# Local attention of a sandwich block on Trainium2: values projected with Wv times Wo, q and k for 256 tokens at a time, norms of four blocks at once

## The reference

```python
x  = hidden_states
gates = sigmoid(x @ Wg + bg);  gates /= gates.sum(-1) + 1e-6
win = xw[:, widx]                         # windows of 64 tokens, one every 32
q, k, v = win @ Wq + bq, win @ Wk + bk, win @ Wv + bv
win_ctx = softmax(q k^T / 4) @ v          # reshaped to rows, first L rows kept
combined = concat(comp_out * g0, sel_out * g1, win_out * g2)
out = norm(0.5 * (combined @ Wo + bo) + 0.5 * x)
```

## Time and profile before

| | |
|---|---|
| median of 3 runs | 1918.43 us (1913.34 to 1921.14) |
| profiled execution | 1920.51 us, span 1918.7 us |
| busy PE, DVE, ACT, POOL | 1676.2, 1261.9, 926.7, 908.5 us |
| TensorE's mean granted clock | 0.941 of full |
| HBM | 18 GB/s over the span |

### The profile page before, as it was taken

How to read it: one execution, slowest core, us unless ns; L and a number is a source line. 1 busy time by engine, 2 the same in 40 slices (tenths; PEclk the granted TensorE clock), 3 DMA queues, 4 the chain that set the end, 5 groups by cost and what they waited for, 6 DMA issues and landing times.

```text
span 1918.7 us, 37804 instructions
## 1 busy us (share of the span) xinstructions
PE 1676.2 (87%) x10522; PEld 1285.8 (67%) x10522; DVE 1261.9 (66%) x3658; ACT 926.7 (48%) x2530; POOL 908.5 (47%) x1070
## 2 busy tenths in 40 slices
PE   3778677999289999999969999399999999789997
PEld 1222366887168787787757778277787877678876
DVE  3666342766478778787645555388788887656765
ACT  1110112554268778788821222178778787711211
POOL 4100031666465555555435554465555555346665
PEclk8788787999699999999989999699999999989999
DMA  4100001021300000000010000200000000001011
GB/s 120 61 1 0 1 0 46 31 68 66 90 3 6 5 4 5 5 4 5 6 60 11 9 8 11 63 4 6 5 4 5 5 4 5 8 23 44 22 43 44
DMA packets 53430, 43.79 MB, mean 23 GB/s; under 512 B 9580, under 2 KB 51840, under 8 KB 53376
## 3 DMA queue, kind: packets, MB, share of 16 engines
q1 hardware_dynamic: 53376, 43.15, 7.2%
HBM read 26.37 MB, written 8.39 MB: 18 GB/s over the span
## 4 chain that ended last, share of the span: by engine, by line
PE 73%; DVE 6%; SPq 6%; DMA 5%; POOL 4%; issue 3%; ACT 2%; POOLq 1%; DVEq 0%; ACTq 0%; PEldq 0%; PEld 0%
PE bank L1446 7%; PE bank L1532 7%; PE bank L1500 6%; PE bank L1459 5%; PE bank L1374 5%; PE bank L1593 5%; PE bank L1594 5%; PE bank L1595 5%; PE bank L1376 5%; PE bank L1375 5%; SPq L465 4%; PE bank L1398 3%; PE bank L1214 3%; DMA x_in<-in_L_attn_hidden_states 2%; POOL h_lo L743 2%
## 5 line engine op out<-in xcount | busy, mean ns | idle before, releaser
L686 POOL TENSOR_TENSOR rnorm<-sumsq,neg_half 128x8 f32<-128x8 f32 x128 | 210.9, 1648 | 139.8 <-DVE sumsq L1941 139.8
L1008 ACT ACTIVATE prob<-prob,neg_max 128x256 f32<-128x256 f32 x512 | 260.9, 516 | 2.3 <-DVE neg_max L2022 2.2
L1127 ACT ACTIVATE gelu_sb<-bank,b_sb 114x512 f32<-114x512 f32 x96 | 66.2, 689 | 350.8 <-PE bank L1595 350.8
L700 POOL TENSOR_TENSOR qk_cos<-qk_cos,qk_sin 128x512 f32<-128x512 f32 x128 | 163.5, 1278 | 125.3 <-DVE qk_cos L1904 122.9
L784 POOL TENSOR_TENSOR act_lo<-act_full,act_hi 114x512 fp32r<-114x512 f32 x96 | 127.0, 1323 | 177.8 <-PE bank L1610 102.5
L1374 PE MATMUL bank<-wqkv_hi,hT_hi 128*128 128x512 f32 x384 | 177.6, 462 | 3.7 <-DVE hT_lo L1890 1.9
L1593 PE MATMUL bank<-h_hi,w_hi 128*114 128x512 f32 (+1 forms) x384 | 156.5, 407 | 20.9 <-POOL h_lo L743 11.0
L1376 PE MATMUL bank<-wqkv_hi,hT_lo 128*128 128x512 f32 x384 | 154.4, 402 | 0.0
L1375 PE MATMUL bank<-wqkv_lo,hT_hi 128*128 128x512 f32 x384 | 154.0, 401 | 0.0
L1594 PE MATMUL bank<-h_hi,w_lo 128*114 128x512 f32 (+1 forms) x384 | 153.5, 400 | 0.0
L2191 DVE SCALAR_TENSOR_TENSOR act_full<-bank,b_sb,gelu_sb 114x512 f32<-114x512 f32 x96 | 71.0, 739 | 125.4 <-PE bank L1595 125.4
(11 more groups left out here) (225 smaller groups left out, 4224.7 us busy)
## 6 DMA issues: line engine op xcount, KB each, us to landing
x_in<-in_L_attn_hidden_states SPq DMA_DIRECT2D x16, 512.0 KB, 3.4
x_scratch<-x_in SPq DMA_DIRECT2D x8, 512.0 KB, 4.2
f_x<-x_scratch SPq DMA_DIRECT2D x8, 512.0 KB, 4.1
out<-f_y SPq DMA_DIRECT2D x8, 512.0 KB, 3.0
hs_attn<-x_sb SPq DMA_DIRECT2D x16, 254.0 KB
hs_ffn<-x_sb SPq DMA_DIRECT2D x64, 63.5 KB
raw<-in_L_ffn_wqkv SPq DMA_DIRECT2D x2, 1536.0 KB, 6.7
raw<-in_L_ffn_w SPq DMA_DIRECT2D x2, 1364.0 KB
```

Of the source, the lines that this page charges most:

```text
L686: pool.tensor_tensor(rnorm[:, part * HEADS:(part + 1) * HEADS], sumsq[:, which * HEADS:(which + 1) * HEADS], neg_half[:, 0:HEADS], ALU.pow ...
L1008: act.activation(prob[:, h], prob[:, h], ACT.Exp, bias=neg_max[:, h:h + 1], scale=-1.0, accum_out=psums[:, h:h + 1]).then_inc(exped, 1)
```

## The change

1. Before phase 2, `W' = Wv Wo3` (`wp_sb`) and `b' = bv Wo3` (`bp_bc`) are computed once: Wv is turned by PE, copied by ACT, multiplied, and copied. PE waits for it before it goes on. `bv` is loaded once more, as a column.
2. In phase 3 the values are `x W'`, straight from `xnT`, so the product with Wo and its copy fall away, and so does the copy of x. p stays unweighed; gate over row sum multiplies the result when it is added (`win_add_up`).
3. q and k are made in units of 288 tokens (four blocks and 32 more), one unit of q or k and one half of its channels per step.
4. Most buffers are doubled. The loops are written out: 32 + 16 steps, each engine with its own list.
5. Norms: POOL makes the scales for four blocks at once (128x4), and also a shift, minus mean times scale. ACT applies both norms as scale and bias. The sum with x0 is one POOL operation of 128x1024 per group. DVE keeps the moments.
6. SP has three buffers for x0. It stores group g as soon as its sum is made, then shifts group g - 2, then loads x0 of group g + 1.
7. For the first layer the sine table goes into rows of `hs_ffn` instead of `pT`.

```diff
+            sp.dma_start(bv_col[:], col(bv)).then_inc(w_loaded, 16)
...
-            sp.dma_start(x_in[:, 0], group_of(x0_b, 0)).then_inc(x0_loaded, 16)
-            sp.wait_ge(x0_loaded, 16)
-            sp.dma_start(x_in[:, 1], group_of(x0_b, 1)).then_inc(x0_loaded, 16)
-            def move_group(g, i):
+            for g in range(3):
+                sp.dma_start(x0_in[:, g], group_of(x0_b, g)).then_inc(x0_loaded[g], 16)
+            def store_x1(g):
+                sp.wait_ge(x1_made, g + 1)
+                sp.dma_start(group_of(x1_dram, g), x0_in[:, g % 3]).then_inc(x1_stored[g % 3], 16)
+            def move_group(g):
                 sp.wait_ge(x_made, (g + 1) * GB)
-                sp.dma_start(hs_attn[1:P, bass.ds(g * GB + g // GPB, GB), :],
-                             x_sb[0:P - 1, bass.ds(g * GB, GB), P:D]).then_inc(hs_moved, 16)
-                sp.dma_start(hs_attn[0:1, bass.ds(g * GB + g // GPB + 1, GB), :],
-                             x_sb[P - 1:P, bass.ds(g * GB, GB), P:D]).then_inc(hs_moved, 16)
-                sp.dma_start(group_of(x1_dram, g), x_in[:, i]).then_inc(x1_stored, 16)
-            with sp.Fori(0, NG // 2 - 1) as u:
-                for i in range(2):
-                    g = u * 2 + i
-                    move_group(g, i)
-                    sp.wait_ge(x1_stored, 16 * (g + 1))
-                    sp.wait_ge(x0_loaded, 16 * (g + 2))
-                    sp.dma_start(x_in[:, i], group_of(x0_b, g + 2)).then_inc(x0_loaded, 16)
-            move_group(NG - 2, 0)
-            sp.wait_ge(x1_stored, 16 * (NG - 1))
-            move_group(NG - 1, 1)
-            sp.wait_ge(x1_stored, 16 * NG)
+                at = g * GB + g // GPB
+                sp.dma_start(hs_attn[1:P, at:at + GB, :], x_sb[0:P - 1, g * GB:(g + 1) * GB, P:D]).then_inc(hs_moved, 16)
+                sp.dma_start(hs_attn[0:1, at + 1:at + 1 + GB, :], x_sb[P - 1:P, g * GB:(g + 1) * GB, P:D]).then_inc(hs_moved, 16)
+            for g in range(NG + 2):
+                if g < NG:
+                    store_x1(g)
+                if g >= 2:
+                    move_group(g - 2)
+                    if g + 1 < NG:
+                        sp.wait_ge(x1_stored[(g - 2) % 3], 16 * ((g - 2) // 3 + 1))
+                        sp.dma_start(x0_in[:, (g + 1) % 3], group_of(x0_b, g + 1)).then_inc(x0_loaded[(g + 1) % 3], 16)
+            for i in range(3):
+                sp.wait_ge(x1_stored[i], 16 * len(range(i, NG, 3)))
...
-            def x1_norm_root(b):
-                inverse_root(f_mv1[:, 1:2], f_r[:], 1e-5, x1_aggr, b + 1, x1_step, b + 1, x1_root, 1)
-            double_norm_scale(0)
-            double_norm_scale(1)
-            with pool.Fori(0, NB - 2) as b:
-                x1_norm_root(b)
-                double_norm_scale(b + 2)
...
+            def sum_scales(g):
+                i = g % 2
+                pool.wait_ge(m_aggr, GB * (g + 1))
+                if g >= 2:
+                    pool.wait_ge(m_norm, GB * (g - 1))
+                var = m_mv[:, i, :, 1]
+                pool.tensor_scalar(m_t[:, 0], var, 0.25, 1e-6, ALU.mult, ALU.add).then_inc(m_step, 1)
+                pool.tensor_scalar(m_t[:, 1], var, 0.25, None, ALU.mult).then_inc(m_step, 1)
+                pool.wait_ge(m_step, 9 * g + 2)
+                pool.tensor_tensor(m_t[:, 0], m_t[:, 0], neg_half[:, 0:GB], ALU.pow).then_inc(m_step, 1)
...
+            def make_x1(g):
+                pool.wait_ge(m_norm, GB * (g + 1))
+                pool.wait_ge(x0_loaded[g % 3], 16 * (g // 3 + 1))
+                pool.tensor_tensor(x0_in[:, g % 3], x0_in[:, g % 3], xs_st[:], ALU.add).then_inc(x1_made, 1)
+            def x1_scales(g):
+                i = g % 2
+                pool.wait_ge(x1_aggr, GB * (g + 1))
+                if g >= 2:
+                    pool.wait_ge(x_made, GB * (g - 1))
+                pool.tensor_scalar(f_r[:, i], f_mv1[:, i, :, 1], 1e-5, None, ALU.add).then_inc(x1_step, 1)
+                pool.wait_ge(x1_step, 3 * g + 1)
+                pool.tensor_tensor(f_r[:, i], f_r[:, i], neg_half[:, 0:GB], ALU.pow).then_inc(x1_step, 1)
+                pool.wait_ge(x1_step, 3 * g + 2)
+                pool.tensor_tensor(f_shift[:, i], f_mv1[:, i, :, 0], f_r[:, i], ALU.mult).then_inc(x1_step, 1)
+                pool.wait_ge(x1_step, 3 * g + 3)
+                pool.tensor_scalar(f_shift[:, i], f_shift[:, i], -1.0, None, ALU.mult).then_inc(x1_root, 1)
+            for n in range(NB + 16):
+                g, r = divmod(n, GB)
+                if r == 0 and 1 <= g <= NG:
+                    sum_scales(g - 1)
+                if r == 0 and 2 <= g <= NG + 1:
+                    make_x1(g - 2)
+                if r == 1 and 3 <= g <= NG + 2:
+                    x1_scales(g - 3)
...
+            act.activation(bv_rep[:], bv_col[:, :, None].broadcast_to([P, DC, P]), ACT.Copy).then_inc(wp_ready, 1)
+            act.wait_ge(wp_ps, 1)
+            act.activation(wvT[:], bank[:, 2].rearrange("p (c m) -> p c m", c=DC), ACT.Copy).then_inc(wp_ready, 1)
+            act.wait_ge(wp_ps, 2)
+            act.activation(wp_sb[:], bank[:, 3].rearrange("p (c n) -> p c n", c=DC), ACT.Copy).then_inc(wp_ready, 1)
+            act.activation(bp_bc[:], bank[:, 4, 0:D], ACT.Copy).then_inc(wp_ready, 1)
...
-            with act.Fori(0, NB) as j:
-                act.wait_ge(win_pt_ps, j + 1)
-                act.activation(pTw[0:WK, :], bank[0:WK, 4, 0:P], ACT.Copy).then_inc(win_pt, 1)
-                act.wait_ge(win_c_ps, j + 1)
-                act.activation(cTw[:], bank[:, 5, 0:2 * P].rearrange("p (m q) -> p m q", m=DC), ACT.Copy).then_inc(win_c, 1)
-                win_exp(j + 1)
-                win_front(j + 2)
-                win_qk(j + 2)
...
+            for n in range(NB + 16):
+                g, r = divmod(n, GB)
+                if n + 1 < NB:
+                    win_exp(n + 1)
+                if n < NB:
+                    win_turned(n)
+                if n + 5 < NB:
+                    unit_out(n + 5)
+                if 6 <= n < NB + 6 and r >= 2:
+                    b = (n - 6) // GB * GB + 2 * (r - 2)
+                    norm_sum(b)
+                    norm_sum(b + 1)
+                if n >= 14 and r in (0, 1) and (n - 14) // GB < NG:
+                    b = (n - 14) // GB * GB + 2 * r
+                    norm_x1(b)
+                    norm_x1(b + 1)
...
+            for c in range(DC):
+                for m in range(DC):
+                    tr = pe.transpose(bank[:, 2, (c * DC + m) * P:(c * DC + m + 1) * P], wv_sb[:, m, c * P:(c + 1) * P], ident[:])
+            tr.then_inc(wp_ps, 1)
+            pe.wait_ge(wp_ready, 2)
+            for m in range(DC):
+                for c in range(DC):
+                    pe.matmul(bank[:, 3, m * D:(m + 1) * D], wvT[:, c, m * P:(m + 1) * P], wo3_sb[:, 2 * DC + c], start=(c == 0), stop=(c == DC - 1))
+            for c in range(DC):
+                mm = pe.matmul(bank[:, 4, 0:D], bv_rep[:, c], wo3_sb[:, 2 * DC + c], start=(c == 0), stop=(c == DC - 1))
+            mm.then_inc(wp_ps, 1)
+            pe.wait_ge(wp_ready, 4)
...
+            def unit(k):
+                h, u = divmod(k, 4)
+                m = u % DC
+                w_sb = (wq_sb, wk_sb)[u // DC]
+                if k >= 2:
+                    pe.wait_ge(win_qk, k - 1)
+                for c in range(DC):
+                    mm = pe.matmul(bank[:, k % 2, 0:UT], w_sb[:, c, m * P:(m + 1) * P], xnT[:, c, token(4 * h):token(4 * h) + UT],
+                                   start=(c == 0), stop=(c == DC - 1))
+                mm.then_inc(win_qk_ps, 1)
...
-            with pe.Fori(0, NB) as j:
-                pe.wait_ge(win_p, j + 1)
-                pe.transpose(bank[0:WK, 4, 0:P], pw[:], ident[:]).then_inc(win_pt_ps, 1)
-                win_values(j + 1, 0)
-                pe.wait_ge(win_pt, j + 1)
-                for m in range(DC):
-                    mm = pe.matmul(bank[:, 5, m * P:(m + 1) * P], vw[0:WK, m * P:(m + 1) * P], pTw[0:WK, :], start=True, stop=True)
-                mm.then_inc(win_c_ps, 1)
-                win_values(j + 1, 1)
-                win_scores(j + 1)
-                win_qk(j + 2)
-                pe.wait_ge(win_c, j + 1)
-                pe.wait_ge(win_add, 1 + j)
-                for m in range(DC):
-                    mm = pe.matmul(bank[:, 6, 0:D], cTw[:, m], wo3_sb[:, 2 * DC + m], start=(m == 0), stop=(m == DC - 1))
-                mm.then_inc(win_o, 1)
+            for n in range(NB):
+                if n + 1 < NB:
+                    win_scores(n + 1)
+                if n + 5 < NB:
+                    unit(n + 5)
+                win_turn(n)
+                if n + 1 < NB:
+                    win_values(n + 1)
+                win_out(n)
...
+                dve.tensor_tensor(w_max[:, j % 4, 1:2], w_max[:, j % 4, 3:4], gate[:, j % BPB, j // BPB, 2:3], ALU.mult).then_inc(win_g, 1)
...
                 dve.wait_ge(win_o, j + 1)
```

(46 more changed lines are left out.)

265 lines of the change are left out of this document (129 added, 136 removed).

## The result

The changed kernel takes 1947.64 us in the median of 4 runs (1946.24 to 1950.87), the kernel before 1919.79 in those beside it (1913.34 to 1922.93): a ratio of 1.0149, 95% interval 1.0129 to 1.0169. It is slower by 1.5%; 1944 and slower were forecast. The profiled execution has a span of 1946.9 us, 28.2 longer than before.

The account below looks back on a forecast made before the run. In the window phase, the x0 load behind SP's slow one-engine shift was taken to set the pace, not PE. 1920.5 + 16.9 (phase) + 8.0 (product) + 0.8 (bias load) = 1946.2, against the median 1944; 8-in-10 range 1930 to 1962.

Parts of the forecast that it names:

- sum for the phase: Window (local attention) phase: first sum, seven loops and tail together 214.0 us against 197.1 before, 16.9 longer.
- First sum, 41.0: Phase start to POOL's first x0 addition: prologue 7.4, nine steps of 2.9 (26.1), then POOL's chain 7.5 us.
- Two loops of 19.0: First two group loops, set by DVE and POOL: 18.1 us plus 0.9 for PE's clock, bounds 17.1 and 21.
- Five loops of 19.3: Groups 3 to 7, set by SP's queue from sum through store, shift and load: 19.3 us each, bounds 18.3 and 20.2.
- Tail 38.5: After group 7's sum, SP stores it and shifts groups 5, 6 and 7 in turn: 38.5 us, bounds 37 and 40.
- Product 8.0: Ahead of the phase, Wv times Wo delays PE's 512-wide products by 8.0 us, nothing hiding it; bounds 6.6 and 9.3.
- bv_col, 0.8: Ahead of the phase, one more bias load in SP's queue before the third x load: 0.8 us.
- rival 1: Window phase: the DVE and POOL loop sets the pace at 21 us; 42 us more in all, 1960; chance 15%.
- rival 3: Window phase: written-out code arrives late, or unpriced waits lengthen each step by 0.7 us; 1966; chance 5%.
- rival 4: Window phase and ahead of it: all low ends together, phase 200.7 us; 1929, about no change; chance 8%.
- Rival 2: Window phase: the shift spreads over more engines than one, shortening tail and last five loops; 1904 (1899 to 1909); chance 8%.
- The signs: New profile: shifts of 10 to 12 us, sums 19 to 20 apart, engines idle 15 to 20 at the end, PE about 60%.

Follow-up runs that it names:

- e1: Changed kernel with the window phase's shift of 127 partitions split into transfers of 112 and 15 partitions; 1894.08 us, ratio 0.9869.
- e4: Changed kernel with SP's load of group g+1 put ahead of the shifts of group g-2; 1924.59 us, ratio 1.0021.
- e6: Changed kernel with SP's shifts of group g-2 put ahead of the store of group g; 1918.65 us, ratio 1.0003.
- e5: Changed kernel with POOL's addition for group g-2 put ahead of the scales of group g-1; 1929.17 us, ratio 1.0062.
- e3: Changed kernel with the product of Wv and Wo moved into the first job's attention, under the softmax; 1935.35 us, ratio 1.0089.

## Why the prediction was right, point by point

- **Time and sign.** 1944 forecast, 1947.64 measured. The sum for the phase was 214.0, it is 216.7; ahead of it 8.8, there are 10.1, and behind it 1.5 less than before. The path is the forecast one: SP's queue with the slow shift holds the last five loops and the tail (e1 takes both away, e4 and e6 move them by order alone). The close number is partly luck: the first sum and the two loops were priced 5.1 us too high, the five loops and the tail 7.8 too low.
- **First sum, 41.0: 39.6.** Steps were 2.9, they are 2.82. POOL's chain was 7.5; it is 4.39 for the scales and 2.34 for the addition, 6.8 with what lies between.
- **Two loops of 19.0: 17.1.** The mechanism is right (e5 removes it). The term was 1.9 too large: 0.7 of POOL's chain, 0.3 of the steps, and 0.9 for a loss by PE's clock. The clock does fall as forecast, behind 3.9 us of idle time, and PE runs at 0.50 from 367 to 370 us (the timeline of PE and a window, third column from the end the granted clock):

```profile
366.73 1.22 PE L1368 MATMUL bank<-vw,pTw 96*128 96x256 f32 x2 [3.91 <-ACT pTw L911]
```

```profile
368.00:369.00 1.00, 1.00 (x5) 0.93 (x5) 0.22 (x3) 0.04 (x1) 0.00 (x0) 0.50 0.00 0
```

  It costs the loop next to nothing: DVE reaches the moments of the four blocks 1.81, 4.40 and 2.82 us apart, so it catches up on blocks that stood ready and loses that time again in the slow stretch. From a sum to DVE's next last moments it is 10.4 us, what steps of 2.82 need.
- **Five loops of 19.3: 20.4.** The term that was too small, by 5.6 us in all: the second shift's row is 11.4 to 11.9 (11.05 with my half microsecond for the store ahead of it) and the load lands in 4.60 to 5.0 (4.2).
- **Tail 38.5: 40.7.** The store's issue is 0.44 (0.6). The three shifts take 39.9 to the last landing, where I had 37.9 (2.2 and 3 x 11.9): 12.77 behind the store, 12.01, and 15.10 for the last, whose landing comes 14.30 behind its last issue. From there to the load of `wo_sb` it is 0.4, which I had not counted.
- **Product 8.0: 7.95** here, 8.0 to 9.0 over six profiles (e3 shows that all of it was exposed).
- **bv_col, 0.8.** The profiles can't tell it: the row ahead of the product starts at 80.10 (78.74 before), but between 76.87 and 80.10 in ten kernels with that load.
- **Rivals.** The loop of DVE and POOL at 21 (rival 1) and late code (rival 3) didn't come; of rival 4's low ends only the two loops of 17.1 did. Rival 2, the shift spread over the engines, was priced at 1904 with an end at 1899; e1 made it so and got 1894, since its loops shorten at the end and mine did not. What I did not see ahead is the size of what the two queue orders cost: SP holds a shift that is ready until a later group's sum, and POOL holds an addition behind a later group's scales.
- **The signs.** Shifts of 11 to 12 us, three of them behind the last sum, and additions that wait for the load from group 3 on came as told. Sums were to be 19 to 20 us apart and are 17.1 and 20.4. The engines' idle time at the end was to be 15 to 20 us and is 22.6:

```profile
519.00:541.60 22.60, 0.00 (x0) 0.00 (x0) 0.00 (x0) 0.00 (x0) 0.00 (x0) 0.50 0.07 21
```

  PE was to be at about 60% in the phase; it is at 48% (104.1 of 216.7 us). My own steps, 32 of 2.9 us, would have given 43% of 214.
- **Slips in the working.** DVE's terms for a step add up to 2.73, not 2.65, and rival 4's first sum to 38.8, not 38.0; the first touches bounds only, the second that rival only. The 3.4 us that I set against POOL's addition came from four separate passes of 0.43. DVE's own addition of 128x1024 takes 1.23 us and POOL's 2.34, a factor of 1.9, so the rule of half the speed that the prediction cites holds here and did not ask for 7 us more.
